# GpSimd's subtractions in two halves, and two key products moved ahead of a chunk's down products

## The reference

```
q, k, v = x Wq, x Wk, x Wv     # 32 heads of 8; rope on q and k
gate    = q . mean(k over each chunk of 32 keys); keep own chunk and the best others, 4 in all
o       = softmax(mask(q k / sqrt 8)) v        # causal, and only the chosen chunks
o       = rmsnorm_per_head(o) * w * sigmoid(x Wg1 Wg2)
x       = layernorm(x + o Wo)
h_e     = relu(x W1_e + b1_e)                  # 2 shared experts, 16 routed, 176 wide
x       = layernorm(x + x + sum shared + sum over top-4 experts of gate_e (h_e W2_e + b2_e))
```

## Time and profile before

| | |
|---|---|
| median of 3 runs | 1563.69 us (1562.2 to 1566.65) |
| the profiled execution: time, span | 1564.33 us, 1562.6 us |
| mean granted clock of TensorE | 0.932 of full speed |
| busy: TensorE, VectorE, ScalarE, GpSimd | 89%, 76%, 54%, 35% of the span |

### The profile page before, as it was taken

One profiled execution on the slowest core, in us unless ns is written; L12 is line 12 of the kernel. 1 busy time (PEld: TensorE's weight loads), 2 busy tenths in 40 slices (PEclk: granted clock), 3 DMA queues, 4 the chain that ended last, 5 costly groups with the idle time before them and its releaser, 6 DMA issues.

```text
span 1562.6 us, 29670 instructions
## 1 busy us (share of the span) xinstructions
PE 1387.1 (89%) x11024; PEld 755.2 (48%) x11024; DVE 1180.3 (76%) x3027; ACT 846.1 (54%) x1266; POOL 539.8 (35%) x638
## 2 busy tenths in 40 slices
PE   5588899898998989989999899989899899999697
PEld 3322575435643466434654257544664346542364
DVE  7994778867786778967788777876789677885634
ACT  5408663385725765276642957348562776428221
POOL 4204432254323542244422543235322443224143
PEclk8758899998999989999999989999899999998799
DMA  6000021100221012111221002210112101220031
GB/s 239 8 15 8 28 76 64 39 29 29 76 68 35 15 56 75 48 29 29 69 68 43 19 24 82 68 30 28 49 62 68 29 15 61 71 48 15 14 103 60
DMA packets 52212, 77.83 MB, mean 50 GB/s; under 512 B 6322, under 2 KB 26724, under 8 KB 51812
## 3 DMA queue, kind: packets, MB, share of 16 engines
q1 hardware_dynamic: 52068, 75.94, 16.4%
HBM read 67.00 MB, written 8.65 MB: 48 GB/s over the span
## 4 chain that ended last, share of the span: by engine, by line
PE 52%; DVE 19%; issue 10%; ACT 9%; POOL 5%; DVEq 3%; DMA 1%; POOLq 1%; SPq 0%
PE PS L564 12%; PE PS L552 10%; PE PS L704 7%; POOL hp L1029 5%; PE PS L481 4%; DVE CM L1314 4%; ACT UQ L973 3%; PE PS L498 3%; ACT hp L834 3%; DVE hr L1125 2%; PE PS L714 2%; PE PS L760 2%; ACT UK L973 2%; PE PS L401 2%; PE PS L451 2%
## 5 line engine op out<-in xcount | busy, mean ns | idle before, releaser
L1029 POOL TENSOR_TENSOR hp<-hr,hp 128x512 f16<-128x512 f32 (+1 forms) x200 | 234.8, 1174 | 637.0 <-ACT hp L834 605.1
L1314 DVE TENSOR_REDUCE CM<-PS 128x32 f32<-128x1024 f32 x320 | 382.1, 1220 | 47.6 <-PE PS L481 45.1
L564 PE MATMUL PS<-W,hp 128*128 128x256 f16 (+1 forms) x2400 | 322.2, 278 | 26.5 <-POOL hp L1029 23.9
L552 PE MATMUL PS<-x1T,W 128*128 128x512 f16 (+1 forms) x1200 | 315.1, 390 | 0.0
L564 PEld LDWEIGHTS PS<-W,hp 128*128 128x128 f16 (+1 forms) x2400 | 216.4, 99 | 124.4 <-POOL hp L1029 65.0
L825 ACT ACTIVATE hr<-PS,CF 128x512 f32<-128x512 f32 (+1 forms) x200 | 137.3, 686 | 207.4 <-PE PS L552 195.8
L834 ACT ACTIVATE hp<-hr 128x512 f16<-128x512 f32 (+1 forms) x178 | 112.5, 632 | 227.7 <-DVE hr L1125 226.0
L1125 DVE TENSOR_TENSOR hr<-hr,gB 128x512 f32<-128x512 f32 x176 | 121.1, 688 | 84.5 <-ACT hr L825 81.2
L973 ACT ACTIVATE UK<-PS 128x1024 f32<-128x1024 f32 x160 | 152.8, 1036 | 29.0 <-PE PS L498 28.0
L552 PEld LDWEIGHTS PS<-x1T,W 128*128 128x128 f16 (+1 forms) x1200 | 108.8, 101 | 114.9 <-issue 39.7
L973 ACT ACTIVATE UQ<-PS 128x1024 f32<-128x1024 f32 x160 | 151.8, 1044 | 5.2 <-PE PS L498 3.4
(11 more groups left out here) (151 smaller groups left out, 1959.4 us busy)
## 6 DMA issues: line engine op xcount, KB each, us to landing
gB<-gates SPq DMA_DIRECT2D x64, 256.0 KB, 3.2
gB<-gates SPq DMA_DIRECT2D x32, 224.0 KB, 2.8
gB<-gates SPq DMA_DIRECT2D x32, 192.0 KB, 2.8
gB<-gates SPq DMA_DIRECT2D x32, 160.0 KB, 2.5
xT<-in_xT SPq DMA_DIRECT2D x8, 512.0 KB, 3.7
qET<-rows SPq DMA_DIRECT2D x16, 256.0 KB, 5.8
v<-in_x SPq DMA_DIRECT2D x8, 512.0 KB, 4.1
gB<-gates SPq DMA_DIRECT2D x32, 128.0 KB, 2.8
```

Of the source, the lines that this page charges most:

```text
L552: mm = pe.matmul(PS[0:w, BK_H[c % 2], :], W1[:, a, k, bass.ds(f0, w)], x1T[:, e, k, :], start=(n == 0), stop=(n == 5))
L564: mm = pe.matmul(PS[:, BK_Y + j // 2, (j % 2) * D:(j % 2 + 1) * D], hp[0:w, slot, a, j * P:(j + 1) * P], W2[0:w, e, bass.ds(c, 1), :].rear ...
L1029: nc.gpsimd.tensor_tensor(hp[0:w, slot, 1, :], hr[0:w, slot, :], hp[0:w, slot, 0, :], ALU.subtract).then_inc(pool_hp, 1)
L1314: nc.vector.tensor_reduce(dst, src, AX.X, ALU.max).then_inc(dve_cm, 1)
```

## The change

GpSimd's `low` and the low parts of E are issued as two instructions, each over half of the columns or heads; the semaphore is raised by the second alone. `late_down(NC - 1)`, the 12 down products of the last chunk, moves from before the waits for the rows and the output gate to behind the first two key units.

```diff
@@ -680,7 +680,6 @@
                 if m is not None:
                     late_down(NC - 2)
-                    late_down(NC - 1)
 
                 pe.wait_ge(s_rows, 64 * (b + 1))
                 pe.wait_ge(act_eg, 2 * b + 2)
@@ -725,7 +724,11 @@
-                for d in range(NU):
+                for d in range(2):
+                    unit(0, 0, d)
+                if m is not None:
+                    late_down(NC - 1)
+                for d in range(2, NU):
                     unit(0, 0, d)
                 group(1, 1)
@@ -1026,8 +1029,10 @@
                 pool.wait_ge(s_high, m * NC + c + 1)
-                nc.gpsimd.tensor_tensor(hp[0:w, slot, 1, :], hr[0:w, slot, :], hp[0:w, slot, 0, :],
-                                        ALU.subtract).then_inc(pool_hp, 1)
+                for s0 in (0, D):
+                    ins = nc.gpsimd.tensor_tensor(hp[0:w, slot, 1, s0:s0 + D], hr[0:w, slot, s0:s0 + D],
+                                                  hp[0:w, slot, 0, s0:s0 + D], ALU.subtract)
+                ins.then_inc(pool_hp, 1)
@@ -1042,8 +1047,10 @@
-                        ins = nc.gpsimd.tensor_tensor(e4[:, :, lo:lo + step + 1:step, :], src,
-                                                      e4[:, :, hi:hi + step + 1:step, :], ALU.subtract)
+                        for h0 in (0, H // 2):
+                            hs = slice(h0, h0 + H // 2)
+                            ins = nc.gpsimd.tensor_tensor(e4[:, hs, lo:lo + step + 1:step, :], src[:, hs],
+                                                          e4[:, hs, hi:hi + step + 1:step, :], ALU.subtract)
                     ins.then_inc(pool_e, 1)
```

## The result

The changed kernel takes 1571.46 us (median of 7 runs, 1567.48 to 1572.12) against 1563.69 before. The ratio is 1.0041 with a 95% interval of 1.0029 to 1.0053: slower by 0.4%, where 1560.6 was forecast and the range ended at 1570. The span of the profiled execution is 1569.7 us, 7.1 more than before, although TensorE's mean granted clock was higher (0.940 against 0.932).

A forecast was written before the change was run, and what follows sets the result against it. TensorE was taken to hold half the chain of waits, with GpSimd's `low` (5%) also on it. The parts summed to a 3.1 us gain on the profiled 1564.33, so 1561.2, or 1560.6 as median; range 1552 to 1570.

The forecast's parts named there:

- step f: Two key units ahead, from SyncE's issue through the groups: ScalarE starts 0.67 us earlier, part kept; +1.0 us (-7 to +4).
- step c: Stacking stretch: longer `low` passed on at every second chunk, one second half delayed behind VectorE; -3.5 us (-1.5 to -7).
- d: Maxima: six `low`s on the chain a turn, each 0.10 us longer; -4.2 us (-1.7 to -5.5).
- g: Turn 0 and the tail: in the tail only its last `low` counts; -0.2 us together.
- e: Row maxima behind the maxima: two VectorE instructions gain 0.5 us each, ScalarE's order caps it at 0.9 a turn; +6.3 us.
- b: Router: VectorE gets 0.9 to 1.4 us back, bounded by TensorE's idle time; +3.7 us (0 to +5).
- Sharing between the engines: VectorE gets in between GpSimd's halves; its instruction of length w delays the second half by w - 0.22 us.
- Rival C: No gap between the halves, so b and e vanish; sum -4.9, 1568.6 us; chance 0.10.
- The second instruction: Fixed cost of splitting a GpSimd operation: 0.04 to 0.13 us, taken as 0.10.
- rival B: Waits in maxima and stacking: GpSimd's latency decides, 0.19 us a split, deciding from about 0.15; 1568.7 us; chance 0.16.
- Rival D: The second instruction costs almost nothing (0.04 us); sum +7.8, about 1556 us; chance 0.26.
- Rival A: `finish` late, its small operations waiting as before, ScalarE stalls; -6.3 us in place of +1.0, about 1568; chance 0.12.

The follow-up runs named there:

- e2: Kernel before with `low` and L1045 (low parts of E) both in halves, without the move of the 12 down products: 1558.95 us, ratio 0.9979.
- e1: Kernel before with only the last chunk's 12 down products moved behind two key units, all GpSimd operations whole: 1577.72 us, ratio 1.0088.
- e12: Changed kernel with one key unit instead of two ahead of the last chunk's 12 down products, no early copy: 1575.83 us, ratio 1.0075.
- e9: Kernel before with only the first copy (L1334) put ahead of the four scalings that end `finish`: 1564.31 us, ratio 1.0006.
- e5: Changed kernel with the first copy (L1334) put ahead of the four scalings that end `finish`: 1555.65 us, ratio 0.9958.
- e10: Kernel before with `low` of the last three chunks and E in halves, plus the first copy ahead of `finish`'s scalings, no move: 1554.86 us, ratio 0.9945.
- e7: e10 plus the move of the 12 down products behind two key units: 1544.65 us, ratio 0.9885 against the kernel before.

## Why the prediction was wrong, point by point

The forecast was a gain of 3.1 us, the traces show a loss of 7.1. Of these 10.2 us, 7.5 are step f and 3.5 step c; d adds 1.6 and g 1.0, and e (2.9) and b (0.5) came out better.

- **Sharing between the engines: right.** VectorE gets in between the halves. A 0.43 instruction beside a pair made it 1.48 instead of 1.29, +0.19 for the 0.2 forecast; a 0.69 one made it 1.75, +0.46 for 0.47. Rival C falls. The Trainium skill (SBUF — State Buffer, "Who interferes with whom") would have the whole instruction added, 0.43 and 0.69; these two rows are against that, for the time that the records show. (The prediction priced that rule at 0.14 a place; by its own w and w - 0.22 it is 0.22, so 4.6 us and not 3. Neither was part of the sum.)
- **The second instruction** costs 0.14 us, not 0.10: beyond my own bound of 0.13, and just short of rival B's point of 0.15. Rival D falls. Rival B's loss in the stacking (7) came out, but its sum does not: with the splits alone (e2) the kernel is faster than before, and B had it 5 us slower.
- **d)** -5.8 for -4.2: six waits of 0.14 are 0.84 a turn, measured 0.8. Only the price was off.
- **c)** -7.0 for -3.5, the end of its range. I had let every second `low` pass its 0.10 on. The whole microsecond of the turn is there: the pair of 597.50 already starts 0.67 before the old one of 598.17 where the turn had been 1.06 ahead, and the pair of 601.29 loses the 0.46 in full.
- **e)** +9.2 for +6.3: the two VectorE instructions gained 0.49 and 0.48, as worked out, and ScalarE's order did not cap it at 0.9. SyncE issues 2.74 us behind L666 instead of 4.03. Part of that is only moved from d: L666 itself comes later, so d and e together are the safer reading, +3.4 for +2.1.
- **b)** +4.2 for +3.7 in this pair of traces, but runs without E in halves differ from before by -0.7 to +4.0 in this stretch, so the agreement shows little.
- **f) is the step that failed: -6.5 for +1.0.** Its first half held: the unit comes 2.8 us behind the issue, for 2.88, and +7.7 came of it. Its second half said that the small operations of `finish` "fall past the three selections and wait 0.5 less; so L1334 starts at about 686.85", 10.64 behind the first key unit. It started 11.66 behind it. The small operations did wait less: 7.25 from the start of `finish` to the scalings, 7.88 before. But `finish` began 2.06 and not 1.85 behind the unit, and the four scalings, which I had left at their 1.38, met selections and took 2.26 (2.03 to 2.65 in other turns). I had taken single-input instructions of that size as free of GpSimd. Behind them the copy had no slack left, `to_tokens` waited 1.0 to 2.1, and ScalarE's fourth exponential 0.8 to 2.8. The trace of before could have told both. The slack of 0.49 was turn 3's alone: the copy's wait for TensorE was 0.60, 2.19, 0.49, 0.09, 0.64, 0.09 and 2.02 us in turns 1 to 7, so in turns 4 and 6 there was next to none, and the seven turns do not repeat each other here. And in turns 4, 5 and 6 the last scaling met a selection and took 0.72 instead of 0.41. Turn 4 of before:

```profile
867.44 1.70 DVE L1155 TENSOR_SCALAR x1n<-x1n,rep 128x256 f32<-128x256 f32 x4
869.23 0.69 DVE L1334 COPY ropeb<-PS 128x512 f32<-128x512 f32 x1
```

Rival A named this place and, with -6.3, nearly the size; I gave it 0.12. That its size came so near is in part luck: A let the small operations wait as long as before, which they did not; the scalings alone took 0.88 more in turn 3, and the clock was not in A at all, nor was a gain of up to 1.9 at the first key unit.
- **What I had no term for:** in each turn of the changed kernel TensorE's granted clock is low for some microseconds of the groups. Where that falls behind the late copy, it adds 1.5 us between the first copy and the second; where it falls ahead, VectorE's lateness hides it. e1 has it behind in all seven turns and loses 21.6, the changed kernel in three and loses 14.2, e12 in three and loses 17.8.
- **g)** -1.2 for -0.2. What is lost is the tail's, and I had no term for it. From its first transposes of x1 on it is 2.2 us longer than before; it is 1.8 and 1.7 longer in the traces of e1 and e9 too, whose tails are the old one, and no longer in that of e2, whose tail has the splits. So the splits are not what lengthened it.

Open: what decides on which side of the copy the clock falls. In e5, without the wait, four of seven turns show no low clock in the groups at all; that the waits bring it about would fit, but before and e2, which wait there little, have it in several turns too.

## What to carry to other kernels

Before an operation of the slack owner is delayed, walk the whole chain behind it to the instruction another engine waits for, and price each of its instructions at the stretch where it will then lie, the contended ones first; here five instructions in another order turned a move that lost about 10 us (e2 to the changed kernel) into one that gains 9 (e10 to e7). Read the slack in every turn and not in one. Work that fills a wait (12 products while a DMA is in flight) delays little there; moved behind the wait, it delays all that waits for it in full (`finish` began 1.84 and 2.06 us behind the first key unit instead of 0.11), and it depends on the slack there whether that costs. Split a helper's instruction only where another engine waits within its length; everywhere else the second instruction's fixed cost is added at each point where someone waits for the whole.

## What the runs showed of the hardware

- Two GpSimd subtractions of 128 x 256 take 1.29 us, one of 128 x 512 takes 1.15.
- VectorE's `TENSOR_SCALAR` with one SBUF input of 128 x 256 waits for GpSimd's selections. In these two traces one takes 0.41 us alone, and 0.51 to 0.85 where a GpSimd instruction began up to 0.14 us before it or within 0.07 us behind its start; the four took 1.38 in turn 3 of before, where they fell between two runs of selections, 1.70 in its turns 4 to 6, and 2.03 to 2.65 in the changed kernel. The Trainium skill (SBUF — State Buffer, "Who interferes with whom") counts `tensor_scalar` among the operations that can, under conditions, enter a two-port mode and so contend with GpSimd; the trace agrees in that they contend. Whether it is this mode the durations do not tell.
- From SyncE's issue of the rows' DMA to the first key unit it is 2.79 to 2.88 us wherever TensorE waited for it, in turn 0 and in turns with experts alike.
